# Half sums of the weighted corners on VectorE, half as many transposes on TensorE, and a norm's scratch values in PSUM

## The chip, the core and the metric

The kernel runs on one core of one Trainium2 chip. The metric is the device time of one execution in microseconds (us). The kernel before takes 20082.83 us, the median of 3 runs (20066.47 to 20095.76).

## The reference, cut to what matters

The input is 32 images of 96 channels and 48 x 48 pixels. Two layers follow each other, each a residual block with a norm over the channels, a mixer and a small quantized feed-forward net.

- Layer 0's mixer is a selective scan: a 1x1 projection and a depthwise 3x3 convolution, then the pixels are sorted by how like they are to the centre pixel, a state-space recurrence runs over them in both directions, and they are put back in their places.
- Layer 1's mixer is a deformable 3x3 convolution. A plain convolution gives for each pixel and each of 9 taps an offset (dy, dx) and a mask. The tap's sample is read between pixels, from the four corners around its position:

```
samp = ((1-wy)*(1-wx)*v00 + (1-wy)*wx*v01 + wy*(1-wx)*v10 + wy*wx*v11) * mask
out  = out + einsum('bchw,oc->bohw', samp, weight[:, :, i, j])      # for the 9 taps (i, j)
```

v00 and v01 are the corners of the upper row, v10 and v11 those of the lower one.

## The kernel before, in words

There are two passes over all images, with a short stretch for batch statistics between them.

Pass one (`pass_one`, the first 11.1 ms of the trace) does layer 0's mixer. It works on four images at a time, each in another phase: the norm and input convolution of one, the sorting of a second, the scan of a third, the end of a fourth. The order of each engine's work is written out by hand as a loop over 72 steps (`for s in range(STEPS)`), with semaphore waits between the engines. A step of the scan has on VectorE (DVE) one multiplication into PSUM (`drives`, L1055) and one scan instruction (`recurrence`, L1071), and on GpSimd (POOL) one multiplication `hc = h * crep` with both operands in SBUF (L1269). Into the same loop on DVE go, between the two, `normalise` (six chunks of an image, from step 46 on, three instructions L1101, L1103 and L1106 each) and `order` (the likeness to the centre pixel, in steps 6 to 14, L1118 to L1138). POOL's queue holds, besides L1269, two scattering or gathering DMAs a step for 9 steps each (L1239, L1257). `inv` and `newton` are slices of the SBUF tile `work`, `rlen` and `dist` small SBUF tiles.

Pass two (`pass_two`, the rest) does the gating, both feed-forward nets and the deformable convolution. Its program covers up to four images, and loops. An image has 18 tiles of 128 pixels. The order of every engine's work is a loop over places (w, u): a period w treats one chunk of 384 pixels (3 tiles, 6 periods an image), and its 12 units u hold the pieces of several chunks in different phases. A tile of the deformable convolution takes four units:

- POOL gathers its corners (L1495): 9 indirect DMAs, one a tap, each bringing for 128 pixels the four corners of 96 channels, 384 values. They go to one of four slots of the tile `G` (`GRING`). A slot may be refilled when the tile that it held has been turned: POOL waits for the semaphore `p_tturn`. The first gather of an image also waits until all DMAs that write this image's table of corners (SP, L1470) have landed (`p_store`).
- DVE multiplies the corners by their weights, in place in `G`, weights in PSUM (`multiply`, L1784): 4 taps in the tile's unit 0, the other 5 in unit 1, each followed by `p_prod`.
- PE turns each weighted corner (128 pixels x 96 channels) into channels x pixels by a transposing matmul, and sums the four corners of a tap in PSUM by accumulation (`turn_samples`, L1514). Per tile these are 9 x 4 = 36 matmuls, each with its own weight load: 16 in the first unit of the next tile, 16 in its second, 4 in its third.
- ScalarE (ACT) copies each group from PSUM to `cols` (`columns`, L1665), and in unit 3 of a period PE multiplies nine taps by the weights (`convolve`, L1528).

Beside it in the same queues run the other pieces of the period: on DVE `normalize` (L1798), `biased` (L1806), `residual` (L1813, L1815), `take` (L1793, after `multiply` in unit 5), xflat (L1835), mix (L1840), x_t (L1852). Norm, hidden layer and output of the feed-forward net form a chain PE, ACT, DVE, PE through most of a period. Weights of 12 tiles at a time lie in PSUM bank `BW`; `set_weights` overwrites them once `p_prod` says that their last use is done.

Of the kernel before, what the change touches and what calls it, by code (L numbers as in the profile page):

```python
# [72 lines left out]
def build_program(nc, I, out, B=IMAGES):  # L73

    with ExitStack() as top:
# [281 lines left out]
        with ExitStack() as loop:  # L357
# [10 lines left out]
                     "p_wset", "p_prod", "p_tturn", "p_cols", "p_conv", "p_x3",  # L368
# [105 lines left out]
def pass_one(nc, ps, S, M, Wt, dram, e_image, s_image, o_image, n_image):  # L474
# [90 lines left out]
    with nc.Block() as block:  # L565
# [466 lines left out]
        def _(dve):  # L1032
# [63 lines left out]
            def normalise(s):  # L1096
                c, part = sub_chunk(s, NORM, 3)
                if c is not None and part == 2:

                    dve.wait_ge(S["n_inv"], c + 1)  # L1100
                    step(dve.scalar_tensor_tensor(out=newton, in0=ps[0:C, BS, 0:CH], scalar=1e-6, in1=newton,  # L1101
                                                  op0=ALU.add, op1=ALU.mult))
                    step(dve.scalar_tensor_tensor(out=newton, in0=newton, scalar=-3.0, in1=inv,  # L1103
# [3 lines left out]
                                             in1=newton.rearrange("p (r x) -> p r x", x=W), op0=ALU.mult,  # L1107
# [5 lines left out]
            def order(s):  # L1113
                rlen, flag, dist = M["rlen"], M["flag"], M["dist"]
                across = lambda ap: ap.unsqueeze(2).to_broadcast([P, ap.shape[1], C])
# [3 lines left out]
                if s == O_DIST + 4:  # L1119
                    dve.wait_ge(S["o_root"], 1)  # L1120
                    step(dve.tensor_scalar(rlen[:], rlen[:], 1e-12, None, ALU.max))

                    dve.tensor_scalar(flag[:], rlen[:], 1e-12, None, ALU.is_le)
                    step(dve.reciprocal(rlen[:], rlen[:]))
                    step(dve.tensor_tensor(unit[:], rows[:], across(rlen[:]), ALU.mult))
# [4 lines left out]
                if s == O_DIST + 7:  # L1130
                    dve.wait_ge(S["o_diffsq"], 1)
                    step(dve.tensor_reduce(dist[:], unit[:, 0:NT, :], AX.X, ALU.add))
                if s == O_DIST + 8:

                    step(dve.tensor_tensor(dist[:], dist[:], flag[:, 0:NT], ALU.add))

                    step(dve.tensor_scalar(flag[:, CEN_TILE:], flag[:, CEN_TILE:], -1.0, 1.0, ALU.mult, ALU.add))
                    dve.tensor_scalar(dist[:], dist[:], flag[:, CEN_TILE:], None, ALU.mult).then_inc(S["o_dist"], 1)  # L1138
# [179 lines left out]
def pass_two(nc, ps, S, M, Wt, dram, parity, stages, has, image):  # L1318
# [124 lines left out]
    with nc.Block() as block:  # L1443
# [60 lines left out]
        def _(pe):  # L1504
            def turn_samples(t, part):
# [6 lines left out]
                for k in range(4 * part, min(4 * part + 4, TAPS)):  # L1512
                    for q in range(CORNERS):
                        m = pe.matmul(ps[0:C, BT + n % 2, (k % 4) * P:(k % 4 + 1) * P],  # L1514
                                      M["G"][:, slot(t - 1), k, q * C:(q + 1) * C], ident[:], is_transpose=True,
                                      start=(q == 0), stop=(q == CORNERS - 1))
# [243 lines left out]
        def _(dve):  # L1760
# [5 lines left out]
            def set_weights(r, t0, t1, used):  # L1766

                sets[0] += 1
                if used:
                    dve.wait_ge(S["p_prod"], 2 * used)  # L1770
                dve.tensor_copy(ps[:, BW, weight_at(t0):weight_at(t0) + (t1 - t0) * TAPS * CORNERS],
                                M["wts"][side(r)][:, t0:t1].rearrange("p t k q -> p (t k q)")).then_inc(S["p_wset"], 1)
                dve.wait_ge(S["p_wset"], sets[0])

            def multiply(g, half):

                t = g % NT
                if half == 0 and g >= AHEAD:
                    dve.wait_ge(S[f"p_got{slot(g)}"], 16 * TAPS * landed(g))
                k0, k1 = (0, SPLIT) if half == 0 else (SPLIT, TAPS)  # L1780
                rows = M["G"][:, slot(g), k0:k1].rearrange("p k (q c) -> p (k q) c", c=C)
# [3 lines left out]
                                  ALU.mult).then_inc(S["p_prod"], 1)  # L1785
# [138 lines left out]
```

## Time and profile before

| | |
|---|---|
| median of 3 runs | 20082.83 us |
| profiled execution, its own time | 20018.78 us |
| its span, first to last instruction | 20017.0 us |
| PE busy (matmul) | 78% |
| DVE busy | 64% |
| POOL busy | 59% |
| ACT busy | 45% |
| mean granted TensorE clock | 0.842 of full speed |

The slices of the profile show two parts: up to slice 22 of 40 DVE is the busiest engine (8 tenths), behind it PE has 7 to 8 tenths, DVE 4 and the DMA engines 5. A busy share is a mean over a stretch. The starts of matmuls are recorded, their ends are modelled, so what PE has truly finished is to be read from the instruction of another engine that was waiting for it.

### The profile page before, as it was taken

How to read it: one execution, taken by the hardware profiler on the slowest of the kernel's cores; microseconds unless marked ns; L12 is line 12 of the kernel's file. 1: busy time of each engine (PE TensorE's matmuls, PEld its weight loads, DVE VectorE, ACT ScalarE, POOL GpSimd, SP SyncE). 2: the span in 40 equal slices, each digit the busy share in tenths (PEclk: the TensorE clock that was granted, in tenths of full speed). 3: DMA queues.
4: the chain of work that ended last, by engine and by line, in shares of the span. 5: the costliest groups of instructions: out<-in, count | busy, mean ns of one | idle time of the engine just before them, and what ended most of it. 6: DMA issues, size and time to landing. Idle time of an engine off the chain costs nothing. (4 is left out here: it accounts for less than half of the span.)

```text
span 20017.0 us, 209117 instructions
## 1 busy us (share of the span) xinstructions
PE 15629.4 (78%) x66607; PEld 8553.2 (43%) x66607; DVE 12801.9 (64%) x14009; ACT 9046.5 (45%) x16414; POOL 11736.7 (59%) x9604
## 2 busy tenths in 40 slices
PE   7878787878787878878787577787777788777777
PEld 3333333333333333333333245455445455454444
DVE  5888888888888888888888244444444444444443
ACT  4555555555555555555554233333333333333332
POOL 3666666666666666666666355555555555555555
PEclk8888888888888888888888688888888888888888
DMA  2333333333333333333333355455545555545554
GB/s 63 88 92 88 88 88 90 87 90 90 90 88 88 88 92 88 88 90 86 92 86 94 96 143 147 141 147 145 144 139 146 143 148 145 143 142 142 146 143 123
DMA packets 1294733, 2230.67 MB, mean 111 GB/s; under 512 B 712841, under 2 KB 756125, under 8 KB 1281629
## 3 DMA queue, kind: packets, MB, share of 16 engines
q1 hardware_dynamic: 893022, 1086.35, 21.2%
q0 software_dynamic: 368640, 1076.24, 18.7%
q10 hardware_dynamic: 32256, 56.64, 0.9%
q8 instruction: 580, 9.50, 0.2%
q14 instruction: 235, 1.93, 0.0%
HBM read 1493.27 MB, written 271.92 MB: 88 GB/s over the span
## 5 line engine op out<-in xcount | busy, mean ns | idle before, releaser
L1495 POOL DMA_INDIRECT G<-corners,idx x5184 | 4920.3, 949 | 3981.5 <-issue 1511.6
L1269 POOL TENSOR_TENSOR hc<-h,crep 128x768 f32<-128x768 f32 x2304 | 4177.6, 1815 | 3747.3 <-DVE h L1071 2255.5
L710 PE MATMUL ps<-hc,sel 128*96 128x512 f32 (+1 forms) x9216 | 3959.7, 558 | 593.0 <-POOL hc L1269 433.9
L1514 PE MATMUL ps<-ident,G 128*96 128x128 f32 x20736 | 2939.7, 298 | 259.6 <-issue 116.0
L1055 DVE TENSOR_TENSOR ps<-dxr,ps 128x768 f32<-128x768 f32 x2304 | 2186.1, 949 | 1372.2 <-PE ps L699 1271.6
L1514 PEld LDWEIGHTS ps<-ident,G 128*96 128x96 f32 x20736 | 2628.4, 139 | 789.3 <-issue 705.2
L1071 DVE TENSOR_TENSOR_SCAN h<-decay,carry,ps 128x768 f32<-128x768 f32 x1536 | 2776.4, 1808 | 164.4 <-ACT decay L893 95.0
L710 PEld LDWEIGHTS ps<-hc,sel 128*96 128x96 f32 x9216 | 1551.8, 184 | 2538.7 <-issue 1787.0
L1784 DVE TENSOR_TENSOR G<-G,ps 128x1536 f32<-128x1536 f32 (+1 forms) x1152 | 2235.7, 1942 | 1.1
L893 ACT ACTIVATE decay<-dtr,a_neg 128x768 f32<-128x768 f32 x2304 | 2120.2, 926 | 229.9 <-DVE h L1071 209.7
L699 PE MATMUL ps<-bq,pick 96*128 96x512 bf16 (+1 forms) x4608 | 1280.4, 363 | 1123.2 <-DVE h L1071 781.7
L1798 DVE TENSOR_TENSOR xq<-ps,rs 96x384 fp8e5<-96x384 f32 x384 | 212.6, 554 | 2576.4 <-ACT rs L1679 2211.1
L1665 ACT ACTIVATE cols_t<-ps 96x512 f32<-96x512 f32 (+1 forms) x1728 | 836.0, 484 | 1939.6 <-PE ps L1514 1073.4
L1528 PE MATMUL ps<-cols_t,w_def 96*96 96x384 f32 x3456 | 1427.6, 578 | 356.1 <-ACT prow L1716 329.0
L790 PE MATMUL ps<-xcp,w_local 96*96 96x384 f32 x3456 | 1545.4, 572 | 3.3 <-ACT local_c L965 1.4
L1071 DVE TENSOR_TENSOR_SCAN h<-decay,ps 128x768 f32<-128x768 f32 x768 | 1341.1, 1746 | 60.2 <-ACT decay L893 33.7
L901 ACT ACTIVATE carry<-h 128x1 f32<-128x1 f32 x1536 | 304.5, 198 | 2288.3 <-DVE h L1071 2223.9
L740 PE MATMUL ps<-xnp,w_conv 97*96 97x384 f32 x3456 | 1251.9, 499 | 4.9 <-ACT x_in L930 2.5
L1671 ACT ACTIVATE sq<-ps 96x384 f32<-96x384 f32 x576 | 280.5, 487 | 2121.2 <-PE ps L1535 1174.9
L699 PEld LDWEIGHTS ps<-bq,pick 96*128 96x128 bf16 x4608 | 387.9, 104 | 1938.2 <-DVE h L1071 1027.8
L1528 PEld LDWEIGHTS ps<-cols_t,w_def 96*96 96x96 f32 x3456 | 653.8, 194 | 1055.6 <-issue 665.8
L1813 DVE TENSOR_SCALAR z<-y,b2q 96x384 f16<-96x384 f16 x384 | 120.9, 315 | 1509.6 <-ACT y L1743 1086.3
(215 smaller groups left out, 21854.0 us busy)
## 6 DMA issues: line engine op xcount, KB each, us to landing
crep<-c_rows SPq DMA_DIRECT2D x3072, 96.0 KB
dtr<-rel SPq DMA_DIRECT2D x2304, 96.0 KB
dxr<-mag SPq DMA_DIRECT2D x2304, 96.0 KB
corners<-prow SPq DMA_DIRECT2D x1536, 72.0 KB
G<-corners,idx POOLq DMA_INDIRECT x5184
x_in<-in_x SPq DMA_DIRECT2D x32, 864.0 KB
local_all<-local_c ACTq DMA_DIRECT2D x192, 144.0 KB
sim<-sorted_rows SPq DMA_DIRECT2D x32, 864.0 KB, 6.1
```

The costliest lines, as they stand in the source:

```text
L699: m = pe.matmul(wide(bank_of(("step", s)), P)[:, a:b], Wt["pick"][:, ng, :], bq[:, q % 2, a:b], start=True, stop=True)
L710: m = pe.matmul(wide(BY, C)[:, a:b], Wt["sel"][:, cg, :], hc[:, v % HC, a:b], start=(v % ROUND == 0), stop=(v % ROUND == ROUND - 1))
L740: m = pe.matmul(ps[0:C, BV, 0:CH], Wt["w_conv"][:, t, :], xn[0:C + 1, 8 * c + t // 3:8 * c + t // 3 + 8, t % 3:t % 3 + W], start=(t == 0), ...
L790: m = pe.matmul(ps[0:C, BV, 0:CH], Wt["w_local"][:, t, :], xpad[:, 8 * c + t // 3:8 * c + t // 3 + 8, t % 3:t % 3 + W], start=(t == 0), st ...
L893: act.activation(decay[:, s % 3, :], dtr[:, q % 2, cg, :], ACT.Exp, scale=Wt["a_neg"][:, direction(q)[0], ng, cg:cg + 1]).then_inc(S["s_de ...
L1055: dve.tensor_tensor(drive, dxr[:, q % 2, cg, :], drive, ALU.mult).then_inc(S["s_drive"], 1)
L1071: dve.tensor_tensor_scan(along(h[:, v % HR, :], k), along(decay[:, v % 3, :], k), along(wide(bank_of(("step", v)), P), k), first, ALU.mult ...
L1269: pool.tensor_tensor(hc[:, s % HC, :], h[:, s % HR, :], crep[:, g % CRING, :], ALU.mult).then_inc(S["s_weighted"], 1)
L1495: pool.indirect_dma_start(M["G"][:, slot(g), k, :], None, dram["tables"][side(r)], bass.IndirectOffsetOnAxis(M["idx"][side(r)][:, t, k:k + ...
L1514: m = pe.matmul(ps[0:C, BT + n % 2, (k % 4) * P:(k % 4 + 1) * P], M["G"][:, slot(t - 1), k, q * C:(q + 1) * C], ident[:], is_transpose=Tru ...
L1528: m = pe.matmul(ps[0:C, BN, 0:CH], Wt["w_def"][:, k, :], M["cols"][:, of_e(w)[1] % 2, k, :], start=(k == 0), stop=(k == TAPS - 1))
L1784: dve.tensor_tensor(rows, rows, by.to_broadcast([P, (k1 - k0) * CORNERS, C]), ALU.mult).then_inc(S["p_prod"], 1)
```

## The change

Pass two: after `multiply`, a new function `halve` on DVE adds the lower row's two weighted corners to the upper row's two, in place in `G` (`rows[:, :, 0:2C] += rows[:, :, 2C:4C]`): for the first four taps in the tile's unit 1, for the other five in unit 2, always behind what else the unit has on DVE except `take`. `p_prod` is now its signal, and `multiply` signals the new `p_mul`. `turn_samples` turns and accumulates the two half sums per tap in place of four corners. Gathers, weights and `columns` stay.

Pass one: the intermediate value of `normalise` is written to the PSUM bank that holds the variance (`var`) in place of the SBUF slice `newton`. In `order`, the length's bounded value and reciprocal (`length`) and the distances (`apart`) are kept in free columns of the same bank until the last instruction writes `dist`.

```
+                    var = ps[0:C, BS, 0:CH]
+                    step(dve.scalar_tensor_tensor(out=var, in0=var, scalar=1e-6, in1=newton,
                                                   op0=ALU.add, op1=ALU.mult))
+                    step(dve.scalar_tensor_tensor(out=var, in0=var, scalar=-3.0, in1=inv,
                                                   op0=ALU.add, op1=ALU.mult))
                     dve.scalar_tensor_tensor(out=centred, in0=centred, scalar=-0.5,
-                                             in1=newton.rearrange("p (r x) -> p r x", x=W), op0=ALU.mult,
+                                             in1=var.rearrange("p (r x) -> p r x", x=W), op0=ALU.mult,
...
+                length, apart = ps[:, BS, CH:CH + NT + 1], ps[:, BS, CH + P // 2:CH + P // 2 + NT]
-                    step(dve.tensor_scalar(rlen[:], rlen[:], 1e-12, None, ALU.max))
-                    dve.tensor_scalar(flag[:], rlen[:], 1e-12, None, ALU.is_le)
-                    step(dve.reciprocal(rlen[:], rlen[:]))
-                    step(dve.tensor_tensor(unit[:], rows[:], across(rlen[:]), ALU.mult))
+                    step(dve.tensor_scalar(length, rlen[:], 1e-12, None, ALU.max))
+                    dve.tensor_scalar(flag[:], length, 1e-12, None, ALU.is_le)
+                    step(dve.reciprocal(length, length))
+                    step(dve.tensor_tensor(unit[:], rows[:], across(length), ALU.mult))
...
+                    step(dve.tensor_reduce(apart, unit[:, 0:NT, :], AX.X, ALU.add))
+                    step(dve.tensor_tensor(apart, apart, flag[:, 0:NT], ALU.add))
+                    dve.tensor_scalar(dist[:], apart, flag[:, CEN_TILE:], None, ALU.mult).then_inc(S["o_dist"], 1)
...
-                    for q in range(CORNERS):
+                    for q in range(CORNERS // 2):
                         m = pe.matmul(ps[0:C, BT + n % 2, (k % 4) * P:(k % 4 + 1) * P],
                                       M["G"][:, slot(t - 1), k, q * C:(q + 1) * C], ident[:], is_transpose=True,
-                                      start=(q == 0), stop=(q == CORNERS - 1))
+                                      start=(q == 0), stop=(q == CORNERS // 2 - 1))
...
-                    dve.wait_ge(S["p_prod"], 2 * used)
+                    dve.wait_ge(S["p_mul"], 2 * used)
...
                 dve.tensor_tensor(rows, rows, by.to_broadcast([P, (k1 - k0) * CORNERS, C]),
-                                  ALU.mult).then_inc(S["p_prod"], 1)
+                                  ALU.mult).then_inc(S["p_mul"], 1)
+
+            def halve(g, half):
+                dve.wait_ge(S["p_mul"], 2 * nth(of_tile, g) + half + 1)
+                _, _, rows = corners(g, half)
+                dve.tensor_tensor(rows[:, :, 0:2 * C], rows[:, :, 0:2 * C], rows[:, :, 2 * C:4 * C],
+                                  ALU.add).then_inc(S["p_prod"], 1)
...
                 if of_tile(t) is not None and sub < 2:
                     multiply(t, sub)
+                if of_tile(t) is not None and 1 <= sub < 3:
+                    halve(t, sub - 1)
```

## Rows read from the trace of the kernel before

**Rows 1.** The page: busy us (share of the span) and instructions by engine.
```profile
PE 15629.4 (78%) x66607; PEld 8553.2 (43%) x66607; DVE 12801.9 (64%) x14009; ACT 9046.5 (45%) x16414; POOL 11736.7 (59%) x9604
```

**Rows 2.** Windows, pass one and pass two: stretch, length, busy time, clock, DMA share, GB/s.
```profile
4000.00:8000.00 4000.00, 3198.87 (x11753) 1534.61 (x11752) 3355.36 (x3111) 2115.73 (x3371) 2518.23 (x1631) 0.87 0.35 89
12500.00:19500.00 7000.00, 5498.17 (x27778) 3499.44 (x27779) 2989.36 (x4447) 2608.10 (x5799) 3955.93 (x4168) 0.82 0.51 144
```

**Rows 3.** The instructions of one line, `take`: one in each period of pass two.
```profile
L1793 DVE SCALAR_TENSOR_TENSOR x<-ps,cols,x x192: 607/607/615, 11405.0 to 20000.3; 96x384 f32<-96x384 f32 x192
```

**Rows 4.** Waits of POOL, 12500 to 19500 us: total us, times, longest.
```profile
POOL G L1495 <- issue: 1233.1, 3741, 16.4
POOL G L1495 <- PE ps L1514: 1172.2, 302, 9.9
POOL G L1495 <- DMA corners<-prow: 392.5, 26, 16.0
POOL G L1495 <- remote: 230.3, 97, 3.8
```

**Rows 5.** Groups by line, 12500 to 19500 us (DVE's with shapes kept apart).
```profile
L1495 POOL DMA_INDIRECT G<-corners,idx x4168 | 3956.4, 949 | 3044.1 <-issue 1233.1 <-PE ps L1514 1172.2 <-DMA corners<-prow 392.5
L1784 DVE TENSOR_TENSOR G<-G,ps 128x1920 f32<-128x1920 f32 x464 | 993.9, 2142 | 0.0
L1784 DVE TENSOR_TENSOR G<-G,ps 128x1536 f32<-128x1536 f32 x464 | 808.4, 1742 | 0.9
```

**Rows 6.** Timeline: start, us, what; 16 turns while no gather is under way.
```profile
15110.26 1.91 PE L1514 MATMUL ps<-ident,G 128*96 128x128 f32 x16
...
15111.78 0.94 POOL L1495 DMA_INDIRECT G<-corners,idx  x1 [15.05 <-DMA corners<-prow]
...
15112.21 0.59 ACT L1665 ACTIVATE cols_t<-ps 96x512 f32<-96x512 f32 x1 [1.26 <-PE ps L1514]
```

**Rows 7.** Timeline: 16 turns while POOL gathers a tile.
```profile
16029.62 1.91 PE L1514 MATMUL ps<-ident,G 128*96 128x128 f32 x16
...
16034.26 0.59 ACT L1665 ACTIVATE cols_t<-ps 96x512 f32<-96x512 f32 x1 [2.07 <-remote]
...
16035.77 0.95 POOL L1495 DMA_INDIRECT G<-corners,idx  x1 [0.30 <-issue]
...
16038.53 0.49 ACT L1743 ACTIVATE y<-ps 96x384 f16<-96x384 f32 x1 [3.67 <-remote]
...
16039.02 0.94 POOL L1495 DMA_INDIRECT G<-corners,idx  x1 [2.30 <-remote]
```

**Rows 8.** Timeline: 16 turns behind an idle stretch of PE.
```profile
16045.38 3.62 PE L1514 MATMUL ps<-ident,G 128*96 128x128 f32 x16
```

**Rows 9.** Timeline of DVE, pass one: tensor_tensor with two SBUF operands.
```profile
5037.56 2.06 DVE L1125 TENSOR_TENSOR unit<-rows,rlen 128x1824 f32<-128x1824 f32 x1
...
5042.17 1.95 DVE L1127 TENSOR_TENSOR unit<-unit 128x1728 f32<-128x1728 f32 x1
```

**Rows 10.** Timeline of POOL in the same stretch.
```profile
5038.54 1.90 POOL L1257 DMA_INDIRECT cmp<-scan_rows,rank_e  x1 [0.30 <-issue]
...
5042.43 2.54 POOL L1257 DMA_INDIRECT cmp<-scan_rows,rank_e  x1 [0.16 <-issue]
```

**Rows 11.** Groups by line of DVE, 2000 to 10000 us.
```profile
L1103 DVE SCALAR_TENSOR_TENSOR work<-work 96x384 f32<-96x384 f32 x140 | 268.1, 1915 | 4.8
L1101 DVE SCALAR_TENSOR_TENSOR work<-ps,work 96x384 f32<-96x384 f32 x140 | 76.5, 546 | 4.4 <-ACT work L926 4.4
L1121 DVE TENSOR_SCALAR rlen<-rlen 128x19 f32<-128x19 f32 x23 | 78.3, 3403 | 0.0
```

**Rows 12.** Timeline, pass one, around one long L1103: DVE's and POOL's.
```profile
5260.59 2.99 DVE L1103 SCALAR_TENSOR_TENSOR work<-work 96x384 f32<-96x384 f32 x1
...
5261.37 1.79 POOL L1269 TENSOR_TENSOR hc<-h,crep 128x768 f32<-128x768 f32 x1
...
5266.03 1.83 POOL L1269 TENSOR_TENSOR hc<-h,crep 128x768 f32<-128x768 f32 x1 [2.87 <-PE ps L710]
```

More of the change, by code:

```diff
@@ L367, in build_program @@
                      "p_ctr3", "p_sq3", "p_var3", "p_rs3", "p_xq3", "p_lin3", "p_yr3", "p_yb3", "p_y", "p_out",
-                     "p_wset", "p_prod", "p_tturn", "p_cols", "p_conv", "p_x3",
+                     "p_wset", "p_mul", "p_prod", "p_tturn", "p_cols", "p_conv", "p_x3",
                      "p_idx", *[f"p_got{i}" for i in range(GRING)])
@@ L1100, in normalise @@
                     dve.wait_ge(S["n_inv"], c + 1)
-                    step(dve.scalar_tensor_tensor(out=newton, in0=ps[0:C, BS, 0:CH], scalar=1e-6, in1=newton,
+                    var = ps[0:C, BS, 0:CH]
+                    step(dve.scalar_tensor_tensor(out=var, in0=var, scalar=1e-6, in1=newton,
                                                   op0=ALU.add, op1=ALU.mult))
-                    step(dve.scalar_tensor_tensor(out=newton, in0=newton, scalar=-3.0, in1=inv,
+                    step(dve.scalar_tensor_tensor(out=var, in0=var, scalar=-3.0, in1=inv,
                                                   op0=ALU.add, op1=ALU.mult))
@@ L1131, in order @@
                     dve.wait_ge(S["o_diffsq"], 1)
-                    step(dve.tensor_reduce(dist[:], unit[:, 0:NT, :], AX.X, ALU.add))
+                    step(dve.tensor_reduce(apart, unit[:, 0:NT, :], AX.X, ALU.add))
                 if s == O_DIST + 8:
-                    step(dve.tensor_tensor(dist[:], dist[:], flag[:, 0:NT], ALU.add))
+                    step(dve.tensor_tensor(apart, apart, flag[:, 0:NT], ALU.add))
                     step(dve.tensor_scalar(flag[:, CEN_TILE:], flag[:, CEN_TILE:], -1.0, 1.0, ALU.mult, ALU.add))
-                    dve.tensor_scalar(dist[:], dist[:], flag[:, CEN_TILE:], None, ALU.mult).then_inc(S["o_dist"], 1)
+                    dve.tensor_scalar(dist[:], apart, flag[:, CEN_TILE:], None, ALU.mult).then_inc(S["o_dist"], 1)
                 t, _ = sub_chunk(s, O_CMP, 1, NT)
@@ L1773, in set_weights, with corners @@
                 dve.wait_ge(S["p_wset"], sets[0])
+            def corners(g, half):
+                k0, k1 = (0, SPLIT) if half == 0 else (SPLIT, TAPS)
+                return k0, k1, M["G"][:, slot(g), k0:k1]
             def multiply(g, half):
@@ L1779, in multiply @@
                     dve.wait_ge(S[f"p_got{slot(g)}"], 16 * TAPS * landed(g))
-                k0, k1 = (0, SPLIT) if half == 0 else (SPLIT, TAPS)
-                rows = M["G"][:, slot(g), k0:k1].rearrange("p k (q c) -> p (k q) c", c=C)
+                k0, k1, rows = corners(g, half)
+                rows = rows.rearrange("p k (q c) -> p (k q) c", c=C)
                 at = weight_at(t)
```

## The prediction

> **What bounds the kernel now.** I read the page first: PE is busy 78% and DVE 64% of the span [rows 1], which singles out neither. The windows then part the run [rows 2]: in pass one DVE has 3355 of 4000 us (84%) and POOL 63%; in pass two DVE has 2989 of 7000 us (43%), PE 5498 (79%) at 0.82 of full clock, POOL 57%. So DVE has room in pass two and little in pass one.
>
> Next the length of a period: `take` runs once in each, 192 times from 11405.0 to 20000.3 us [rows 3], so a mean period is 8595.3 / 191 = 45.0 us, and pass two is worth 192 of them. 7000 / 45.0 = 155.6 periods lie in the window of the waits.
>
> What fills POOL's 45.0 us? Per period: 27 gathers of 0.949 us, 25.6 [rows 5]; 1233.1 / 155.6 = 7.9 us of issue between them; (1172.2 + 230.3) / 155.6 = 9.0 us waiting for a slot of `G` to be turned (the 97 waits "remote" sit in the same place, as in rows 7); and 392.5 / 155.6 = 2.5 us waiting for the table of the next image [rows 4]. Together 45.0. So the gathers alone would need 36.0 us, and 9.0 us is time in which POOL waits for PE's turns.
>
> Why are the turns late? The timeline shows 16 turns issued in 1.91 us in both of two cases. With no gather under way the copy that waits for them starts 1.95 us after the first (15112.21 - 15110.26) [rows 6]: 0.12 us a turn. While a tile is being gathered it starts after 4.64 us (16034.26 - 16029.62): 0.29 us a turn [rows 7]. And the work behind them is late too: y waits until 16038.53 and the next slot until 16039.02, about when the gathers issued up to 16036.72 have landed [rows 7]. So PE's turns and the gathers hinder each other, a period has 108 turns, and PE is loaded far more than its 79% tells.
>
> The Trainium skill (SBUF — State Buffer, section "SBUF: two separate sides") says that engine and DMA accesses to SBUF cannot contend. These rows speak against it for the turns, whatever the cause. By that rule a turn would cost 0.12 us everywhere and the change would take at most 54 x 0.12 = 6.5 us from a period's PE work, an estimate near the one below.
>
> **Removed from PE.** 36 turns a tile become 18, 108 a period become 54. At 0.12 us each that is 6.5 us a period, at 0.29 us 15.7 us; behind an idle stretch of PE, at half clock, 16 turns take 3.62 us [rows 8], 0.23 each, between the two. Since POOL gathers in 25.6 + 7.9 of 45.0 us, I go by the upper figure for three turns in four: 54 x (0.75 x 0.29 + 0.25 x 0.12) = 13.4 us of PE time. That is more than the 9.0 us POOL waits for, so the turns cease to be the bound and POOL's own queue is what is late next.
>
> **Added on DVE.** `multiply` costs 1.742 us for 1536 values and 2.142 for 1920 [rows 5], so 1.042 ns a value and 0.142 us fixed; two SBUF operands cost the same (1728 values: 0.142 + 1.80 = 1.94, measured 1.95 [rows 9]). `halve` has 4 x 192 = 768 values, 0.94 us, and 960, 1.14 us: 2.08 us a tile, 6.25 a period. DVE goes from 0.43 x 45.0 = 19.2 to 25.5 us of a period, so it is not the bound. On the path it costs less: in unit 5 the first half stands before `take`, for which the next norm waits (0.94), and in units 9 and 10 both stand before `biased`, whose consumer on ACT also has the next norm behind it (at most 2.08). These 3.0 us lie on the chain of the feed-forward net; the 13.4 us gone from PE's queue between its links cover them. Without that cover a period would gain 3.0 us.
>
> The new `p_prod` comes one unit later than the old. PE asks for a half four units after its `multiply`, some 45.0 / 12 x 4 = 15 us, so I cost this wait at nothing; nothing else waits for `p_prod`. `halve`'s wait for `p_mul` is on an instruction that ended before.
>
> **Added on POOL.** `halve` is an addition with two SBUF operands. In pass one such an instruction stretches an indirect DMA that meets it: beside the 1.95 us L1127 one takes 2.54 us, 1.59 more than 0.95; beside L1125 one takes 1.90 us, 0.95 more [rows 9, 10]. Scaled by length, 1.59 / 1.95 = 0.82, six halves a period add 0 to 0.82 x 6.25 = 5.1 us to POOL's queue. They miss the sensitive moment often (the two stretches are 0.46 and 0.82 of their instructions), so I take a third, 1.7 us.
>
> **Period after.** 36.0 + 1.7 = 37.7 us; of the 9.0 us waiting for turns I leave 1.2 us, because PE's chain with 54 turns is near this length too: 38.9 us. Saved: 6.1 x 192 = 1171 us. Ends: nothing stretched, no wait left: 9.0 x 192 = 1730; full stretch and 3 us of waits left: 0.9 x 192 = 170.
>
> **Pass one.** L1103 takes 1.915 us in the mean, its neighbour L1101 with one operand in PSUM 0.546, at the same size [rows 11]. It waits for POOL's L1269 (at 5260.59 it ends 2.99 us later, after the L1269 of 5261.37 to 5263.16 [rows 12]). With `var` in PSUM it has one SBUF operand, and so has L1106. Top of the gain: 1.37 x 192 = 263 us, and L1121 3.40 us against 0.17 for work of that size (estimate from the fixed 0.142): 3.2 x 32 = 103, together 366 us. Bottom 0: where POOL's queue is full behind it, DVE's wait is hidden. In the case shown POOL then idles 2.87 us [rows 12]; of an image's six L1103 I count one such. L1125 loses its second SBUF operand and stretches no gather: 0.95 us [rows 10]. 2.9 + 0.95 = 3.8 us x 32 = 122 us. I take 120. No wait is added.
>
> The Trainium skill has the rule for both (SBUF — State Buffer, same section): DVE with two SBUF inputs and a GpSimd instruction that reads SBUF take the shared pair as "an exclusive lock, not a bandwidth split". By it a gather that meets `halve` would wait for the rest of it every time; that is the second rival.
>
> **Sum.** Profiled execution 20018.8 - 1171 - 120 = 18728 us; the median before is 64 us above its profiled execution, so 18790.
>
> **Rivals.**
> - *The landings pace the period (15%).* If turns of any number are only done when the tile's gathers have landed, as the end of rows 7 looks, a tile takes 9 x 1.25 + 2.0 us (2.30 less the usual 0.30), 13.3, a period 39.9 + 2.5 = 42.4 us: 2.6 x 192 = 499, with pass one 619: 19465. For: y and the slot come free together. Against: the 16 turns in rows 7 were done with gathers still being issued.
> - *Full stretch (13%).* Each `halve` stretches a gather, 5.1 us, and some waits for turns stay: 36.0 + 5.1 + 1.2 = 42.3 us, 2.7 x 192 = 518, with pass one 638: 19445. For: the 2.54 us of rows 10. Against: the 1.90.
> - *Slower (6%).* In pass two the waits of 9.0 us do not depend on the number of turns, and the full stretch comes on top: 45.0 + 5.1, so + 979 - 120: 20940. It decides as soon as the stretch exceeds what the turns give back. Against: the turns with no gather are done in 1.95 us, so their number counts.
> - *It doesn't do what it says (1%).* Pass one's values in PSUM leave L1103 as long, and pass two gains nothing: 20080.
>
> **How the numbers follow.** The forecast has 65%. Its own range is 18350 (1730 would be all of the waits; with 120 it gives 18233, and I leave that tail) to 19300. To hold 8 in 10 with the two rivals near 19450 it goes to 19600. No change means within 0.2%, 40 us, about what a measurement tells apart: faster 0.93, same 0.01, slower 0.06.
>
> **What would show it.** L1514 at 18 a tile; the copies behind turns under a gather about 2.3 us after their start, not 4.6; POOL's waits for L1514 down from 9.0 us a period to some 1 to 2; gathers' mean above 0.949 by 1.7 / 27 = 0.06 us; `halve` 0.94 and 1.14 us; `take` every 38.9 us in the mean; L1103 near 0.55 us. I am wrong if POOL's waits stay above 5 us, or if the gathers' mean rises by 0.15 us or more, or if DVE's chain makes PE wait at `take`.

## The result, and the profile after

The changed kernel takes 19816.4 us, median of 4 runs (19795.8 to 19832.45), against 20089.3 us for the kernel before on the same chip: ratio 0.9866, 95% interval 0.9848 to 0.9883, so 1.34% or 273 us faster. The prediction was 18790 us, range 18350 to 19600: right in sign, four to five times too large, and the time lies above the range. One run of the kernel before in a later series took 24949 us, at a clock of 0.71 in place of 0.84, and is left out of the ratios.

The page after: busy time, share and instructions by engine.
```profile
PE 14796.9 (75%) x56239; PEld 7501.1 (38%) x56239; DVE 13588.7 (69%) x15161; ACT 9075.2 (46%) x16414; POOL 12666.8 (64%) x9604
```
The same two windows as [rows 2], then `take`, once in each period of pass two, as [rows 3]:
```profile
4000.00:8000.00 4000.00, 3179.76 (x11976) 1538.65 (x11975) 3271.51 (x3144) 2163.07 (x3436) 2532.80 (x1647) 0.90 0.36 90
12500.00:19500.00 7000.00, 5015.61 (x19559) 2721.47 (x19557) 3893.24 (x5391) 2638.66 (x5824) 4778.34 (x4198) 0.74 0.51 144
```
```profile
L1806 DVE SCALAR_TENSOR_TENSOR x<-ps,cols,x x192: 604/607/614, 11232.7 to 19796.5; 96x384 f32<-96x384 f32 x192
```
The first `take` stands 172 us earlier than before: that is pass one's gain. Then 191 periods take 8563.8 us, 44.84 us each, where they took 8595.3 us, 45.00: pass two gained 31 us, not 1171. The two profiled runs are 204 us apart and not 273, since the profiled run before lies 70 us below the median of its series. PE's busy time in the window fell by 483 us, 3.2 us a period, and its granted clock from 0.82 to 0.74; 13.4 us a period had been counted on.

POOL's waits, 12500 to 19500 us, as [rows 4], and groups by line there, as [rows 5] (DVE's with shapes kept apart):
```profile
POOL G L1497 <- issue: 1299.5, 3909, 15.7
POOL G L1497 <- PE ps L1516: 377.3, 103, 14.6
POOL G L1497 <- remote: 324.1, 170, 3.6
POOL G L1497 <- DMA corners<-prow: 220.6, 16, 14.6
```
```profile
L1497 POOL DMA_INDIRECT G<-corners,idx x4198 | 4779.3, 1138 | 2221.5 <-issue 1299.5 <-PE ps L1516 377.3 <-remote 324.1
```
```profile
L1797 DVE TENSOR_TENSOR G<-G 128x960 f32<-128x960 f32 x465 | 533.0, 1146 | 0.9
L1797 DVE TENSOR_TENSOR G<-G 128x768 f32<-128x768 f32 x465 | 440.6, 948 | 0.0
```
With 156.1 periods in the window, POOL's 44.8 us are now: gathers 27 x 1.138 = 30.7 us (25.6 before), issue 8.3 (7.9), waits for turns 4.5 (9.0), table 1.4 (2.5). So the waits for turns fell by 4.5 us and those for the table by 1.1, while the gathers grew by 5.1 us and the issue by 0.4.

A gather beside two halves, timeline: start, us, engine and line.
```profile
16027.43 0.95 DVE L1797 TENSOR_TENSOR G<-G 128x768 f32<-128x768 f32 x1
16027.84 2.95 POOL L1497 DMA_INDIRECT G<-corners,idx  x1 [0.30 <-issue]
16028.30 0.61 DVE L1865 SCALAR_TENSOR_TENSOR x_t<-ps,cols,x_t 96x384 f32<-96x384 f32 x1
16028.82 1.14 DVE L1797 TENSOR_TENSOR G<-G 128x960 f32<-128x960 f32 x1
16029.89 1.74 DVE L1790 TENSOR_TENSOR G<-G,ps 128x1536 f32<-128x1536 f32 x1
```
The gather starts in the first `halve` and ends at 16030.79, 0.82 us after the second one's end at 16029.97. The 0.45 us between the two halves, in which DVE had L1865, gave it nothing. That is so throughout: from 12500 to 17500 us 323 gathers meet a `halve` and are longer than 1.1 us, and 318 of them end 0.81 to 0.83 us after the end of the last `halve` that they met. 240 of the 330 pairs of halves there are spanned by one gather each; on chip 7 (run a2 below) it is 346 of 368.

A held gather, then, waits for the end of the addition and needs 0.82 us after it, out of the 0.95 that it takes alone. Nine gathers of a tile grew by 9 x 0.189 = 1.70 us; that 0.82 times a tile's 2.08 us of `halve` gives the same is chance. The Trainium skill (SBUF — State Buffer, section "SBUF: two separate sides") calls the pair "an exclusive lock"; this trace agrees with it here.

Pass one, groups by line of DVE, 2000 to 10000 us, as [rows 11]:
```profile
L1104 DVE SCALAR_TENSOR_TENSOR ps<-ps,work 96x384 f32<-96x384 f32 x144 | 80.9, 562 | 5.0
...
L1123 DVE TENSOR_SCALAR ps<-rlen 128x19 f32<-128x19 f32 x24 | 4.1, 171 | 0.0
...
L1137 DVE TENSOR_TENSOR ps<-ps,flag 128x18 f32<-128x18 f32 x23 | 4.1, 178 | 0.0
```
The norm's second step went from 1.915 to 0.562 us and the `max` on the row lengths from 3.403 to 0.171, as priced. DVE has 6 x 1.35 + 3.2 = 11.3 us less an image; 172 / 32 = 5.4 us of it reach the span. The indirect DMA of pass one (L1257, now L1259) went from 1.135 to 1.084 us in the mean, 0.9 us for an image's 18, where 0.95 had been priced for the operand that L1125 lost.

### The profile page after: what moved, and what is told of

The parts are those of the page before. It is cut to its first block and busy times, and to the rows that moved or that the text cites. A ratio compares the mean times of both kernels' runs of the same rounds, so it can differ in the third digit from the quotient of the medians.

```text
span 19813.4 us, 189542 instructions
## 1 busy us (share of the span) xinstructions
PE 14796.9 (75%) x56239; PEld 7501.1 (38%) x56239; DVE 13588.7 (69%) x15161; ACT 9075.2 (46%) x16414; POOL 12666.8 (64%) x9604
## 5 line engine op out<-in xcount | busy, mean ns | idle before, releaser
L1497 POOL DMA_INDIRECT G<-corners,idx x5184 | 5884.3, 1135 | 2967.6 <-issue 1580.5
L710 PE MATMUL ps<-hc,sel 128*96 128x512 f32 (+1 forms) x9216 | 3883.3, 549 | 642.1 <-POOL hc L1271 488.5
L1530 PE MATMUL ps<-cols_t,w_def 96*96 96x384 f32 x3456 | 1579.4, 627 | 652.0 <-ACT prow L1718 563.7
L1516 PE MATMUL ps<-ident,G 128*96 128x128 f32 x10368 | 1847.8, 329 | 240.7 <-issue 160.6
L1516 PEld LDWEIGHTS ps<-ident,G 128*96 128x96 f32 x10368 | 1537.0, 156 | 789.1 <-issue 673.8
L1530 PEld LDWEIGHTS ps<-cols_t,w_def 96*96 96x96 f32 x3456 | 715.9, 213 | 1444.2 <-issue 854.6
L1797 DVE TENSOR_TENSOR G<-G 128x768 f32<-128x768 f32 (+1 forms) x1152 | 1190.3, 1047 | 1.1
```

The source lines that it names most:

```text
L710: m = pe.matmul(wide(BY, C)[:, a:b], Wt["sel"][:, cg, :], hc[:, v % HC, a:b], start=(v % ROUND == 0), stop=(v % ROUND == ROUND - 1))
L1497: pool.indirect_dma_start(M["G"][:, slot(g), k, :], None, dram["tables"][side(r)], bass.IndirectOffsetOnAxis(M["idx"][side(r)][:, t, k:k + ...
L1530: m = pe.matmul(ps[0:C, BN, 0:CH], Wt["w_def"][:, k, :], M["cols"][:, of_e(w)[1] % 2, k, :], start=(k == 0), stop=(k == TAPS - 1))
```

## Experiments

Theories: S, the additions' two SBUF operands hold up POOL's gathers and eat the gain; C, a fixed order of waits between PE, ACT and DVE sets the period; K, PE's clock falls as it has less to do. Two more came up with the first runs below: L, PE's signals wait for the gathers' landings whatever PE has to do; T, it is the transposing instruction that waits.

The chips turned out to differ. The kernel before takes 19990 us on chip 14 and 20084 on chip 4, but 18114 and 18104 on chip 1, 18113 on chip 7 and 18171 on chip 2. The runs of one kernel on one chip agree within 85 us, the one named above aside, and chip 1 was met in two series with the same time. The other chips were met in one series each, so that it is the chip, and nothing else that held during a series, is likely but not shown. Pass one is as long on both kinds (first take at 11.2 to 11.4 ms); all of the difference is in pass two. I call them slow and quick chips. The first series' chip is not recorded; its times and waits are like those of chips 4 and 14. The period in the table is that of the takes; "wait" is POOL's wait for turns per period (PE and remote, 12500 to 17500 us; for the first two rows to 19500).

```
kernel (turns a period)              chip  ratio to before   period  gather mean  wait
before (108)                         slow  1                 45.00   0.949        9.0
after (54)                           slow  0.9866            44.84   1.138        4.5
b1 before again (108)                14    one run, 20009 us 44.83   0.951        8.8
a1 after again (54)                  14    0.983             43.78   1.138        4.1
e1 pass one's part (108)             4     0.9923            45.42   0.949        9.4
e3 half the turns, no sum (54)       4     0.9847            43.73   0.953        9.0
e4 sum, all turns (108)              4     1.0192            47.50   1.143        7.0
e5 sum with a PSUM operand (54)      14    0.976             43.12   0.952        7.6
e7 reduction (27)                    14    0.9757            43.14   0.953        9.1
e7 reduction (27)                    4     0.9724            43.33   0.956        9.3
e1 pass one's part (108)             1     0.992             35.30   0.960        0.5
e2 pass two's part (54)              1     1.0571            40.71   1.188        0.1
e3 half the turns, no sum (54)       1     0.9966            34.98   0.954        0.3
e4 sum, all turns (108)              1     1.0566            40.58   1.183        0.1
a2 after again (54)                  7     1.0483            40.56   1.181        0.1
e8 after, plain turns (54)           7, 2  1.0478, 1.0457    40.57   1.182        0.0
e9 reduction, plain turns (27)       7, 1  1.0304, 1.0322    39.03   0.962        5.0
e10 before, plain turns (108)        7     1.0775            42.54   0.951        7.6
```

### The parts alone: e1, e2, e3, e4

e1 keeps only the lines of `normalise` and `order`, e2 only those of pass two. e3 and e4 start from the kernel before:

```
e3:  -  for q in range(CORNERS):                 e4:  +  halve(t, sub - 1)   # as in the change
     +  for q in range(CORNERS // 2):                    (turns: all four corners, unchanged)
     (no halve)
```

> The kernel before with pass one's values in PSUM alone, pass two as it was. In the changed kernel the first take of pass two stands at 11232.7 us, 172 us earlier than before, and the takes then follow each other for 8563.8 us in place of 8595.3. If pass one is worth what its own stretch shows, this kernel is 172 us faster than before, about 19915 us. If part of it is lost again at the border of the passes, it is 100 us or less. Were pass two to gain from it as well, it would be above 200 us.

> The kernel before with pass two's part alone: DVE adds the lower row's corners, PE turns and sums two half sums per tap. By the traces of the changed kernel it gains 31 us plus what is left of the 270, so 30 to 100 us: 19990 to 20060 us. My forecast had 1171 us for it. Only if the two parts disturb each other would this kernel alone come near 19000 us.

> The kernel before, but PE turns only the upper row's two corners of each tap, and nobody adds the lower row's: its output leaves out half of every sample. It shows what 54 turns a period are worth without the additions on DVE. Theory S (the additions stretch POOL's gathers by 5.1 us a period, and that eats the gain): the gathers stay at 0.95 us, POOL's waits for turns fall from 9.0 us to about 1 a period, the period goes to some 37 to 39 us, and the time to 18500 to 18950 us. Theory C (a fixed order of waits between PE, ACT and DVE sets the period, and the turns only filled PE's waits): the period stays above 44 us, the time above 19850 us, and POOL's waits stay at 8 to 9 us a period. Theory K (PE idles more, its clock falls, and all its other work takes longer): granted clock at 0.74 or less, the convolution of L1528 at 0.63 us or more in place of 0.578, the time between the two, 19000 to 19800 us.

> The kernel before with the additions on DVE, but PE still turns and sums all four corners (the lower row's count twice, so the output is another one). It shows what the additions cost by themselves. Theory S: the gathers' mean rises from 0.949 to about 1.14 us, POOL's queue gets 5.1 us longer on top of waits for turns that stay, the period goes to 48 to 50 us and the time to 20700 to 21050 us. Theory C: the additions cost at most the 3.0 us that stand before take and biased, so up to 20660 us, and POOL's waits shrink by what the gathers gain in length. Theory K: the clock stays at 0.82 and the time within 1% of before.

All four ran on chip 1, where nothing was as the first trace had it. e1: 17968.5 us against 18113.6, 145 us faster, as expected in size. e2: 5.7% slower (5.5 to 5.9). e3: 0.3% faster. e4: 5.7% slower. The takes of e1 on chip 1, and POOL's waits there, 12500 to 17500 us:

```profile
L1795 DVE SCALAR_TENSOR_TENSOR x<-ps,cols,x x192: 607/607/614, 11252.1 to 17995.3; 96x384 f32<-96x384 f32 x192
```
```profile
POOL G L1497 <- issue: 1221.9, 3757, 15.6
POOL G L1497 <- PE ps L1516: 68.4, 47, 5.6
```
Pass two, unchanged, has a period of 6743.2 / 191 = 35.30 us and half a microsecond of waits for turns. The forecast's 36.0 us for a period without waits for turns is near what this chip does without any change: POOL's queue is its bound, there is no wait that fewer turns could take away (e3), and every microsecond of stretch lies on the path (e2, e4). The line of the gathers in e2, chip 1:

```profile
L1495 POOL DMA_INDIRECT G<-corners,idx x3296 | 3915.5, 1188 | 1081.2 <-issue 1062.9 <-PE ps L1514 14.3 <-DMA corners<-prow 4.0
```
27 x (1.188 - 0.960) = 6.2 us of stretch; the period is 5.4 us longer, since the waits that were there went with it. It also speaks against theory C by itself: with the same order of waits the period is 35.3 us on this chip and 45.4 on chip 4.

What differs between the kinds is seen in the same instructions. In e1 on chip 1, 16 turns with gathers under way, timeline (for [rows 7] of before):

```profile
16024.49 1.91 PE L1516 MATMUL ps<-ident,G 128*96 128x128 f32 x16
...
16024.57 0.95 POOL L1497 DMA_INDIRECT G<-corners,idx  x1 [0.30 <-issue]
...
16025.82 0.95 POOL L1497 DMA_INDIRECT G<-corners,idx  x1 [0.30 <-issue]
...
16026.44 0.59 ACT L1667 ACTIVATE cols_t<-ps 96x512 f32<-96x512 f32 x1 [1.26 <-PE ps L1516]
```
The copy starts 1.95 us after the first turn, exactly as in [rows 6] with no gather; in [rows 7] it took 4.64 us.

The table is worked out from the records of the traces, 12500 to 17500 us. "Signal late": the next signal record of the turns comes over 0.3 us behind the end of the instruction that signals. "Copy late": ScalarE had been idle since the turns' end, and its copy starts over 0.3 us behind it.

```
                            turns a period  signals late   median   copies late   median
before, first series             108        579 of 993     2.5 us   168 of 315    1.2 us
e1, chip 4                       108        625 of 981     2.7 us   171 of 310    1.2 us
e3, chip 4 (run below)            54                                186 of 302    1.1 us
e7, chip 14 (run below)           27                                150 of 301    1.3 us
e1, chip 1                       108          1 of 1269               0 of 707
```
The copies show it without the signals' records, and they are late in 50 to 62% of these cases with 108, 54 or 27 turns. Two limits go with this. The ends of matmuls are modelled, so a late signal and a turn that was truly finished late look the same. And on slow chips signal records are missing: of 1020 for the turns of e3 862 are there, of 993 for those of before 980, of 663 for `multiply` 418; on chip 1 none is. A missing one counts as late, so the column of signals is an upper bound, and left out for e3 and e7. All runs here were recorded by the profiler, and no run tells whether the recording itself has a part in what slow chips do.

On a slow chip other signals of PE are late too, by a rough count 57% of those behind a turn in its queue and 35% of the others. At 59% of the turns' late signals of the first series gather packets pause just afterwards, at most 4 in the next 0.3 us, where 31% of all moments are such.

### The same on a slow chip

> Half of the turns and no addition, on top of the kernel before, once more. The series fell on two chips: on chip 1 the kernel before takes 18114 us, PE's signals follow its instructions by 0.01 us, and half of the turns gained 0.3%; on chip 14 it takes 19990 to 20089 us, and while gathers are under way PE's signals come 1.9 us late in the median, several at once when the packets pause. If that delay grows with the number of turns (a price per turn, as my prediction had it), this kernel gains 6 to 7.8 us a period on such a chip: 18500 to 18800 us. If the signals wait for the gathers' landings whatever PE has to do (theory L), the period stays above 42 us and the time above 19500 us. On a chip like 1 it is 0.3% faster than before again.

> The additions with all four turns a tap, on top of the kernel before, once more. On a chip like 14, theory L: the gathers get 5.1 us longer a period (mean 1.14 us), but POOL had 9 us of waits for turns, which shrink by most of that; the time is 0 to 2% above before, 20000 to 20400 us. With a price per turn, the 9 us stay and the stretch comes on top: 20900 us. On a chip like 1 it is 5.7% slower again.

> Pass one's part alone, once more. On a chip like 14: pass one ends 172 to 210 us earlier (first takes at 11218 to 11242 us in three kernels with it, 11405 and 11428 without), pass two as before: 0.990 to 0.991 of before, about 19800 us; the changed kernel had 0.983 and 0.987, so pass two's part would be worth 0.4 to 0.7% there. On a chip like 1: 0.992 again.

These fell on chip 4. e1: 0.9923 (0.9906 to 0.9939), 153 us; so pass one's part is worth 0.8% on both kinds. e3: 0.9847 (0.983 to 0.9863), 303 us. Both e3 and e4 came out as theory L says and not as a price per turn does. e3's gathers and what ended their waits, chip 4, 12500 to 17500 us:

```profile
L1495 POOL DMA_INDIRECT G<-corners,idx x3068 | 2923.4, 953 | 2077.7 <-issue 916.3 <-PE ps L1514 690.9 <-remote 332.3
```
With 114.3 periods in 5000 us, (690.9 + 332.3) / 114.3 = 9.0 us a period: half of the turns are gone, nothing was added, and POOL still waits for turns about as long as before. What e3 gains against e1 on the same chip, 45.42 - 43.73 = 1.7 us a period, is mostly another wait, that for the next image's table: e1, then e3, same window.

```profile
POOL G L1497 <- DMA corners<-prow: 285.3, 19, 15.9
```
```profile
POOL G L1495 <- DMA corners<-prow: 138.2, 9, 15.9
```
That is 2.6 us a period and 1.2; the waits for turns went from 9.4 to 9.0.

e4: 1.0192 (1.0175 to 1.0209): the gathers stretch by 5.2 us a period, the waits shrink by 2.4 against e1's, and 2.1 us of the period remain as loss against e1. 1.9% is within the 0 to 2% expected under theory L, though the time, 20482 us, lies 82 us above the range given with it; a price per turn had 20900 us.

### The change again, and the sum without the second SBUF operand

```
e5, in halve:  -  in1 = rows[:, :, 2 * C:4 * C]            (SBUF)
               +  in1 = the weights in ps, spread over C   (PSUM), as many values
     (set_weights waits for p_prod again, since the weights are read once more)
```
```
e7:  - dve.tensor_tensor(rows[:, :, 0:2 * C], rows[:, :, 0:2 * C], rows[:, :, 2 * C:4 * C], ALU.add)
     + dve.tensor_reduce(M["sums"][:, k0:k1], rows.rearrange("p k (q c) -> p k c q", c=C), AX.X, ALU.add)
     - for q in range(CORNERS // 2): ... M["G"][:, slot(t - 1), k, q * C:(q + 1) * C]
     + for q in range(1):            ... M["sums"][:, k]
     (the reduction stands one unit later than halve, and waits for p_tturn of the tile before,
      which is turned out of the same buffer)
```

> The kernel before once more, for a second trace. In the runs so far the same kernel took 20089 us in one series and 18114 us in another, on another chip, with pass one equally long in both (the first take at 11.3 to 11.4 ms). With pass two as before and beside it, the takes followed each other every 35.3 us there in place of 45.0, and 16 turns under a gather took 1.95 us in place of 4.3. If this series is like the second, 18110 us, period 35.3 us and POOL's waits for turns under 1 us a period; if like the first, 20080 us, 45.0 and 9.0 us.

> The changed kernel once more. Where the turns are as quick under a gather as without one (16 in 1.95 us), POOL's own queue is the bound before the change, and the change can only lengthen it: the two parts by themselves gave -145 and +1034 us, so about 19000 us against 18114, 4.9% slower. Where the turns are hindered by the gathers (4.3 us), it repeats the first series: 1.3% faster, 19816 against 20089 us.

> The changed kernel, but the second operand of the additions comes from PSUM (the weights again, spread over the channels) in place of the lower row's products in SBUF: as many values, the same place in DVE's order, but one SBUF operand; its output leaves out the lower row's samples. Theory S (the pair of SBUF operands holds up POOL's gathers): the additions still take 0.94 and 1.14 us, but the gathers' mean falls from 1.14 to 0.95 us, and 5.1 us of POOL's queue a period go: 5.1 x 192 = 980 us less than the changed kernel in a series where POOL's queue is the bound. Theory C (it is the additions' length on DVE's queue that costs, not their operands): the time stays within 100 us of the changed kernel and POOL waits instead.

> The changed kernel, but in place of an addition of two SBUF operands one reduction sums all four corners of a tap into a buffer of its own (one SBUF operand, 1536 and 1920 values read, so an estimated 1.74 and 2.14 us by the rate of multiply), one and two units later, and PE turns 9 times a tile in place of 18; the output is the full one. Theory S: the gathers stay at 0.95 us and it is faster than the changed kernel by about 980 us where POOL's queue is the bound, though DVE has 5.4 us more a period (3 x 1.8); where the turns are hindered it gains more, since 27 turns a period are left of 54. Theory C (DVE's length counts): it is slower than the changed kernel by up to 5.4 x 192 = 1040 us.

Chip 14, a slow one. b1 repeats the first trace (44.83 us, waits 8.8). a1: 0.983 (0.981 to 0.985). e5: 0.976 (0.974 to 0.978), and its gathers:

```profile
L1497 POOL DMA_INDIRECT G<-corners,idx x3121 | 2970.1, 952 | 2031.8 <-issue 912.6 <-PE ps L1516 758.2 <-DMA corners<-prow 238.0
```
0.952 us in place of 1.138: the stretch is due to the second SBUF operand and to nothing else of `halve`, since length (0.944 and 1.142 us), place and number are the same. Theory S stands as to the cause. But of the 5.0 us that this takes from POOL's queue only 43.78 - 43.12 = 0.7 us leave the period; the waits for turns go back up from 4.1 to 7.6. e7 has 27 turns a period and waits of 9.1 us:

```profile
POOL G L1498 <- PE ps L1517: 860.8, 217, 22.8
POOL G L1498 <- remote: 193.1, 90, 3.5
```
With gathers at 0.95 us the waits for turns are 9.4 us with 108 turns (e1, chip 4), 9.0 and 7.6 with 54 (e3, chip 4, and e5, chip 14), 9.1 with 27 (e7, chip 14). So on a slow chip they do not follow the number of turns. With the wait for the table they fall a little: 12.0 us, 10.2 and 9.7, 9.5. e7 is a weaker witness than e3, as its turns also come after reductions that keep DVE busy 86% of the time.

> The reduction over all four corners, with 9 turns a tile, once more. On a chip like 14 it is again 0.976 of before. On a chip like 1, where POOL's queue is the bound: the gathers stay at 0.95 us since no instruction of pass two gained a second SBUF operand, DVE's extra 11.6 us a period (43% busy of 45 before, about 86% of 35.3) just fit, and the time is near that of pass one's part alone, 17970 to 18150 us, so 0.992 to 1.0 of before, against 1.05 for the changed kernel there. If DVE becomes the bound instead, the period goes to 37 us or more: over 18250 us.

Chip 4: 0.9724 (0.971 to 0.974), period 43.33. The first branch held. e7 is the fastest version with the full output on slow chips; on a quick chip it was not measured, only e9 below.

### Is it the transposing instruction?

```
e8, e9, e10:  - ..., ident[:], is_transpose=True, start=...
              + ..., ident[:], start=...        (on after, on e7, on before)
```

> The changed kernel, with the turns as plain products with the identity matrix in place of transposing instructions (same reads of G, same writes, same 18 a tile). On chips 4 and 14, where signals come late under gathers, the late ones are the turns' and those of instructions queued close behind them; L1632 and L1537, plain products that follow a wait, are on time. Theory T (it is the transposing instruction that is held while gathers land): the lag goes to 0.01 us, POOL's waits for turns vanish and the period falls from 44.8 to about 41 us (POOL's queue with stretched gathers, 30.7 + 8.3 us, and what is left): 19000 to 19250 us. Theory L (PE's signals wait for the landings whatever the instruction): no gain; a plain fp32 product costs more PE time, so 0 to 3% slower than the changed kernel. On a chip like 1 both say: within 1% of the changed kernel.

> The kernel with the reduction over all four corners and 9 turns a tile, with plain products for the turns. Theory T: gathers at 0.95 us and no wait for turns, so the period falls from 43.1 to 36 or 37 us: 18100 to 18400 us on a chip like 4 or 14. Theory L: 43 us, 19500 us. On a chip like 1: 17950 to 18300 us.

> The kernel before with plain products for all 36 turns of a tile and nothing else changed. Theory T: the 108 turns of a period take about 23 us of PE at an estimated 0.21 us each (by L1630's kind of product) in place of 13, but their signals are on time: period 38 to 43 us, 18700 to 19700 us on a chip like 4 or 14. Theory L: PE's queue gets 10 us longer a period and the signals stay late: 46 to 52 us, over 20300 us. On a chip like 1: between no change and 5 us more a period, 18100 to 19100 us.

> The changed kernel once more, beside the three above on the same chip. On a chip like 4 or 14 0.983 to 0.987 of before; on a chip like 1 about 1.049 of before, 19000 us, since POOL's queue is the bound there and the two parts alone gave 0.992 and 1.057.

Chip 7, a quick one, so theories T and L were not told apart. a2 measures the change on such a chip: 1.0483 (1.0465 to 1.050), 4.8% slower, against 1.049 from the parts. Its takes and gathers:

```profile
L1806 DVE SCALAR_TENSOR_TENSOR x<-ps,cols,x x192: 603/607/614, 11219.2 to 18965.4; 96x384 f32<-96x384 f32 x192
```
```profile
L1497 POOL DMA_INDIRECT G<-corners,idx x3315 | 3916.3, 1181 | 1086.0 <-issue 1070.2 <-PE ps L1516 15.5 <-DMA corners<-prow 0.3
```
e8 equals it. e10 is 7.7% slower: PE is the bound there, by its window (columns as in [rows 2]; 4717 of 5000 us at clock 0.99):

```profile
12500.00:17500.00 5000.00, 4716.82 (x33561) 3689.30 (x33560) 2267.92 (x3362) 1978.74 (x4374) 2989.43 (x3144) 0.99 0.54 152
```
e9 was expected at 17950 to 18300 and took 18672.6 us. Its window and its reduction:

```profile
12500.00:17500.00 5000.00, 3843.81 (x16037) 2150.05 (x16035) 4741.31 (x4441) 2148.41 (x4775) 3299.09 (x3431) 0.79 0.59 166
```
```profile
L1800 DVE TENSOR_REDUCE sums<-G 128x384 f32<-128x1536 f32 x764 | 2376.2, 3123 | 0.7
```
A reduction takes 3.12 us in the mean (2.79 for 1536 values read, 3.46 for 1920) where I had estimated 1.74 and 2.14 from `multiply`; DVE is busy 95% and sets the period of 39.0 us. On chip 14 the same DVE work left the period of e7 where e5 has it, 43.1 us.

> The changed kernel with plain products in place of transposing instructions, once more: on chip 7, where the kernel before takes 18113 us, it was 1.048 of before, as the changed kernel itself is (1.048), and no signal of PE is late in either, so it told nothing apart. On a chip like 4 or 14, theory T (the transposing instruction is held while gathers land): PE's lag at the turns 0.01 us, period about 41 us, 19000 to 19250 us. Theory L (any instruction of PE, or its signal, is held): the lag stays at 1 to 3 us, and the time is 0 to 3% above the changed kernel, 19650 to 20300 us.

> The kernel with the reduction over all four corners and 9 plain turns a tile, once more. On a quick chip (7) it was 1.030 of before with a period of 39.0 us, DVE 95% busy, since a TENSOR_REDUCE of 1536 or 1920 values took 3.12 us in the mean, not 1.94. With transposing instructions the same kernel had a period of 43.1 and 43.3 us on the slow chips 14 and 4, and 0.976 and 0.972 of before. If this series falls on a slow chip: by theory T (the transposing instruction is held while gathers land) PE's signals are on time and DVE is the bound, 39 to 40 us: 18700 to 18950 us, 0.935 to 0.945 of before. By theory L (any instruction of PE, or its signal, is held) the period stays at 43 us: 19450 to 19700 us, 0.97 to 0.98. On a quick chip: 1.030 again.

Both fell on quick chips (2 and 1) and repeated the above: 1.0457 and 1.0322. What holds back PE's signals on slow chips, the transposing instruction or any, stays open, and so does why some chips show it: no plain product was measured on a slow chip.

No version tried beats both kernels everywhere. Pass one's part alone is faster than before on both kinds (0.992) and the best on quick chips; on chips 4 and 14 e7 is (0.972 to 0.976).

## Why the prediction was wrong

- **The bound.** The sum of POOL's 45.0 us was right. The forecast failed at the step that reads "PE's turns and the gathers hinder each other" as a price per turn, 0.29 us under a gather: "54 x (0.75 x 0.29 + 0.25 x 0.12) = 13.4 us of PE time. That is more than the 9.0 us POOL waits for, so the turns cease to be the bound". It took 7.8 of the 9.0 us of waits away. e3 on chip 4 took those 54 turns away without adding anything, and the wait was 9.0 us still, the period 45.42 - 43.73 = 1.7 us shorter. What the 4.64 us of [rows 7] contain is a delay that does not grow with the turns: copies are late as often behind 54 and 27 turns a period as behind 108, and on chip 1 16 turns take 1.95 us under gathers too.
- **How far that explains the wait.** By a rough count from the signals' records, 1.5 of the 8.3 us a period that POOL waits for a turn's signal in the first trace (the usual 0.3 us of issue taken off) are that signal's own lateness, and 3.1 of 7.7 in e3's on chip 4; in the rest the turn itself came late, behind copies and other work of PE. That this is the same delay further up the chain is argued from chip 1, where both are gone, and no run shows it link by link.
- **Added on POOL.** "I take a third, 1.7" us: the traces have 5.1 on the slow chips and about 6 on the quick chips. The reason given, that the halves "miss the sensitive moment often", was a misreading of [rows 9] and [rows 10]. Both stretched DMAs there end alike behind their addition: 5040.44 - 5039.62 = 0.82 us and 5044.97 - 5044.12 = 0.85. The one met by L1125 was stretched less only because it began later in it, 0.98 us after its start and not 0.26. Two halves stand so close together that one gather spans both, and a gather fills 0.95 of each 1.25 us in which POOL issues them, so most pairs meet one. On slow chips this mis-sized term cost only 0.7 us a period (e5), since the gathers' growth took the place of waiting; on quick chips it is the whole loss of 5.3 us.
- **Added on DVE.** 0.948 and 1.146 us against 0.94 and 1.14: right. With the lock gone, e5 gains 1.7 us a period against the unchanged pass two on its chip (44.83 to 43.12), as e3 without any addition does on its own (45.42 to 43.73), so the 3.0 us before `take` and `biased` were covered. DVE's added wait cost nothing that shows.
- **PE's clock** was left out of the sum. PE's busy time fell by 3.2 us a period where 54 turns at 0.12 us are 6.5, and the granted clock of pass two went from 0.82 to 0.74 (e7: 0.66). Part of the freed time went into slower instructions. No run changes the clock alone; but e5 and e7 on chip 14 have the same period at 0.75 and 0.66, and e3 on chip 1 has a shorter one at 0.86 than e1 at 0.94, so nothing here shows it setting the period.
- **Pass one.** 120 us predicted, 172 between the first takes, 153 and 145 by e1. The guess that one L1103 in six shows was too low: by these figures 40 to 48% of DVE's saving showed.
- **Sum and rivals.** 31 + 172 us in the traces' spans of takes, where 1171 + 120 stood. "The landings pace the period", 42.4 us, had 15%; without the stretch (e3, e5, e7) the period is 43.1 to 43.7, the nearest of all, though what holds the turns is shown only as late signals and copies. "Full stretch", 42.3 us, had the stretch right and its waits of 1.2 us wrong: 4.5. "Slower", with the waits independent of the turns and the stretch on top, had the first half right; I summed them, but on slow chips one takes the other's place. On quick chips there is no wait to take, and that rival's sign is what is measured. Of the prediction's signs of being wrong, one came true in the first series: the gathers' mean rose by 0.19 us, over 0.15. POOL's waits, 4.5 us, stayed under its mark of 5, since the stretch had taken their place.
- **Not explained:** Alone, the halved turns gave 1.7 us and the additions cost 2.1 (chip 4, against e1); together they gain 0.2 us (first series) to 1.0 (chip 14). The parts do not add, by up to 1.5 us a period.

## What to carry to other kernels

A wait on an engine is no proof that less work on it shortens the wait. See first whether what it releases comes late by an amount that grows with its work, and price a term by taking the work away with nothing added, as e3 did. An addition of two SBUF operands on DVE, placed beside a queue of indirect gathers, holds a gather until the addition ends and 0.82 us more; give it a PSUM operand where the values can lie there. Pass one's norm got one, and pass one's part gained 0.8% on both kinds of chip. And a gain of 1.3% on one chip was a loss of 4.8% on another: a change that trades one engine's time for another's wants both measured.

## What the runs showed of the hardware

The same program takes 18.1 to 18.2 ms on chips 1, 2 and 7 and 20.0 to 20.1 ms on 4 and 14. Transfers are as quick (a gather packet of 3072 bytes takes 0.124 us in the mean on either kind, by the DMA records), instructions take as long, but copies that wait for turns start over 0.3 us late in about half of the cases on chips 4 and 14 (171 of 310 in e1, 150 of 301 in e7), and in 0 of 707 on chip 1. A TENSOR_REDUCE over four values with a stride of 96 took 3.12 us for 1536 to 1920 values read, 1.6 times the multiplication of as many. And gathers held by one `halve` stay held through the next, 0.45 us later, with another DVE instruction between; they end 0.82 us after the last one's end, and an indirect DMA of pass one ended 0.82 and 0.85 us after additions of 2.06 and 1.95 us that it met 0.98 and 0.26 us after their start.
